# Encoder values made with tokens on the partitions, and their head layout assembled by DMA through DRAM

## The reference, cut to what matters

```python
keys = jnp.concatenate([past, x], axis=1)
q = (x @ Wq.T + bq).reshape(B, T, HEADS, HEAD_DIM)
k = (keys @ Wk.T + bk).reshape(B, T + H, HEADS, HEAD_DIM)
v = (keys @ Wv.T + bv).reshape(B, T + H, HEADS, HEAD_DIM)
...
attn = jax.nn.softmax(scores, axis=-1)
o = jnp.einsum('bhqk,bkhd->bqhd', attn, v).reshape(B, T, C)
o = o @ Wo[l].T + bo[l]
```

## Time and profile before

| what | value |
|---|---|
| time, median of 3 runs | 821.11 us (820.96 to 821.4) |
| span of the profiled execution | 819.1 us |
| TensorE (PE) busy | 801.5 us, 98% of the span |
| VectorE (DVE) busy | 633.9 us, 77% |
| ScalarE (ACT) busy | 460.6 us, 56% |
| GpSimd (POOL) busy | 251.6 us, 31% |
| DMA | 88.36 MB, 30.4% of 16 engines' span |

### The profile page before, as it was taken

How to read it: one execution, slowest core, us unless ns; L and a number is a source line. 1 busy time by engine, 2 the same in 40 slices (tenths; PEclk the granted TensorE clock), 3 DMA queues, 4 the chain that set the end, 5 groups by cost and what they waited for, 6 DMA issues and landing times.

```text
span 819.1 us, 16629 instructions
## 1 busy us (share of the span) xinstructions
PE 801.5 (98%) x6060; PEld 751.4 (92%) x6060; DVE 633.9 (77%) x1287; ACT 460.6 (56%) x829; POOL 251.6 (31%) x297
## 2 busy tenths in 40 slices
PE   9999999999999999999999999999999999999988
PEld 8998789999999999899999989999998999999758
DVE  5786693778778876778797887878778787876796
ACT  4386424433333336585786777667687767745421
POOL 0002120410111100364366147335525623633020
PEclk9999999999999999999999999999999999999999
DMA  5010946998889812010210021031012103010001
GB/s 191 1 52 1 373 124 253 328 323 310 317 309 337 321 53 107 1 40 14 100 44 0 17 98 38 13 102 38 4 39 72 38 13 102 26 82 1 1 0 30
DMA packets 18290, 88.36 MB, mean 108 GB/s; under 512 B 3120, under 2 KB 7472, under 8 KB 12240
## 3 DMA queue, kind: packets, MB, share of 16 engines
q1 hardware_dynamic: 18256, 87.90, 30.4%
HBM read 85.05 MB, written 2.84 MB: 107 GB/s over the span
## 4 chain that ended last, share of the span: by engine, by line
PE 47%; issue 23%; POOL 18%; DVE 8%; ACT 3%; DMA 1%; POOLq 0%; SPq 0%; DVEq 0%; ACTq 0%
PE bank L1139 14%; POOL W_L L2000 7%; PE bank L1176 6%; POOL HF_L L2058 4%; POOL arena L1981 3%; POOL WQKV_L L2000 3%; PE bank L746 2%; PE bank L872 2%; PE bank L1185 2%; PE bank L722 2%; PE bank L1049 2%; PE bank L788 1%; POOL SQ L2019 1%; PE bank L1123 1%; PE bank L1490 1%
## 5 line engine op out<-in xcount | busy, mean ns | idle before, releaser
L1139 PE MATMUL bank<-arena 128*128 (+1 forms) x1024 | 117.8, 274 | 0.0
L1139 PEld LDWEIGHTS bank<-arena 128*128 128x128 f32 x1024 | 117.4, 192 | 0.0
L1981 POOL TENSOR_TENSOR arena<-arena,srec 111x456 f32<-111x456 f32 x56 | 52.3, 962 | 125.1 <-DVE srec L2153 125.1
L2000 POOL TENSOR_TENSOR W_L<-LW,W_H 128x256 fp32r<-128x256 f32 x96 | 68.5, 752 | 36.9 <-DVE XHL L2589 33.5
L2058 POOL TENSOR_TENSOR HF_L<-arena,HF_H 128x296 fp32r<-128x296 f32 x48 | 43.8, 937 | 76.7 <-ACT HF_H L1896 76.7
L788 PE MATMUL bank<-XHL,W_H 128*128 128x296 f32 x288 | 65.1, 307 | 0.0
L1896 ACT ACTIVATE arena<-bank,vec 128x296 f32<-128x296 f32 x96 | 48.8, 509 | 20.4 <-PE bank L788 15.4
L2012 POOL TENSOR_TENSOR QW<-QW,arena x14 | 22.4, 1600 | 119.0 <-DVE QW L2490 65.6
L1330 PE MATMUL bank<-HF_L,W_H 128*128 128x296 f32 x192 | 57.4, 299 | 0.0
L1330 PE MATMUL bank<-HF_H,W_H 128*128 128x296 f32 x192 | 57.4, 299 | 0.0
L1330 PE MATMUL bank<-HF_H,W_L 128*128 128x296 f32 x192 | 57.3, 299 | 0.0
(11 more groups left out here) (276 smaller groups left out, 2205.4 us busy)
## 6 DMA issues: line engine op xcount, KB each, us to landing
arena<-ew_in SPq DMA_DIRECT2D x16, 2048.0 KB, 9.0
arena<-ew_in SPq DMA_DIRECT2D x16, 1024.0 KB, 7.0
LW<-lw_in SPq DMA_DIRECT2D x12, 1024.0 KB, 5.0
arena<-route SPq DMA_DIRECT2D x32, 185.0 KB, 3.2
LW<-lw_in SPq DMA_DIRECT2D x6, 768.0 KB, 4.3
fp_weights<-arena SPq DMA_DIRECT2D x1, 2048.0 KB, 6.4
arena<-fp_weights SPq DMA_DIRECT2D x1, 2048.0 KB, 7.2
arena<-patches_in SPq DMA_DIRECT2D x2, 864.0 KB, 7.4
```

Source lines behind the costliest of these rows:

```text
L1139: last = mm(o[:, m * CAP:(m + 1) * CAP], w[:, kc, mi * P:(mi + 1) * P], xg(kc, e), start=(kc == 0), stop=(kc == C - 1))
L1981: nc.gpsimd.tensor_tensor(v, v, srec[0:QROWS, s:s + 2, :].unsqueeze(3).to_broadcast([QROWS, 2, C * JH, KEYS]), ALU.mult).then_inc(p_ready, 1)
L2000: last = nc.gpsimd.tensor_tensor(low[:, cols], value[:, cols], high[:, cols], ALU.subtract)
```

## The change

V of a half is made token-major: the stationary operand is now 104 token columns of x (13 tokens of 8 images), the moving one the 256 V columns of the weights. For this the columns of the encoder's activations are ordered token by token, image within token (`by_key` in place of `images`), so that 104 neighbouring columns are 13 tokens of all 8 images; three such tiles start at tokens 0, 12 and 24. V takes 18 products with 256 moving columns (`value_rows`), 12 of them ahead of the layer norm's variance and 6 behind it; the 16 transposes, the mask products on VectorE and the threefold copy are gone. Q and K chunk 0 come first, V last. ScalarE copies the rows out of PSUM twice per half (104 rows by 512 and by 256 columns). SyncE then stores them to a DRAM tensor `spread` of [128, 8, 256] that is zeroed once at the start: 9 DMAs per half, one for each of 3 tiles and 3 slots, on 104, 96 and 96 rows, with 6, 5 and 5 runs of 16 numbers (64 bytes) in each row, 4736 runs in all. When they have landed, SyncE loads the whole 1 MB into `Ve` with one DMA, which `values` waits for. The Q/K/V weights of the next layer are issued behind that load. In chunk 1 the head slots are rotated by one (`krot`), since 8 heads are no multiple of 3. `set_kbias` moves into the A phase, behind the softmax sums.

```diff
@@ -120,11 +120,10 @@
-    att("w", 0, 1)
...
         att("k", c)
-    att("v", 0, 1, 2, 3)
+    att("w", 0, 1)
@@ -136,6 +135,10 @@
+KEY_STARTS = (0, 12, 24)
+KEY_RUN = 13
+VROWS = KEY_RUN * HB
@@ -246,6 +250,7 @@
         VT = v_.rearrange("p (c b g k) -> p c b g k", c=C, b=HB, g=JH)
+        v3 = VT.rearrange("p c b g k -> p (c b g k)")[0:VROWS, 0:3 * D].rearrange("p (i n) -> p i n", i=3)
@@ -357,6 +362,11 @@
+        spread = nc.dram_tensor("spread_values", (P, HB, D), F32, kind="Internal").ap()
+        spread_rows = spread.rearrange("r b n -> (r b) n").rearrange("x (e d) -> x e d", d=HD)
+        SPREAD_DMAS = len(KEY_STARTS) * JH
@@ -462,6 +473,10 @@
+        def half_count(l, h):
+            return l * 2 + h
@@ -516,6 +531,9 @@
+        def by_key(ap):
+            return ap.rearrange("p (t b) -> p b t", t=T)
@@ -620,6 +638,8 @@
             sp.dma_start(lvec[:, :, :], a["lvec"].rearrange("l p n -> p l n")).then_inc(ld_lvec, 16)
+            sp.wait_ge(setup_done, 1)
+            sp.dma_start(spread, OB[:, 0, 0, 0:D].unsqueeze(1).to_broadcast([P, HB, D])).then_inc(spread_zeroed, 16)
@@ -691,16 +711,44 @@
-            with sp.Fori(1, LAYERS) as l:
-                sp.wait_ge(filled["v"], nth("v", 7, l))
+            def store_value_rows(l, h):
+                sp.wait_ge(w_ready, nth("w", 2 * h + 1, l + 1))
+                if not (isinstance(l, int) and l + h == 0):
+                    sp.wait_ge(spread_loaded, half_count(l, h) * 16)
+                for i, k0 in enumerate(KEY_STARTS):
+                    lo = 0 if i == 0 else (KEY_STARTS[i - 1] + KEY_RUN - k0) * HB
+                    for g in range(JH):
+                        row = (g * KEYS + k0) * HB
+                        sp.dma_start(spread_rows[row + lo:row + VROWS, g::JH, :],
+                                     v3[lo:VROWS, i, :].rearrange("p (e d) -> p e d", d=HD)[:, g::JH, :]
+                                     ).then_inc(spread_stored, 16)
+            def load_value_rows(l, h):
+                sp.wait_ge(spread_stored, half_count(l, h) * (SPREAD_DMAS * 16) + SPREAD_DMAS * 16)
+                sp.wait_ge(filled["o"], nth("o", 3, l + 1) if h else nth("o", 7, l))
+                sp.dma_start(Ve[:, 0:HB, :], spread).then_inc(spread_loaded, 16)
+            sp.wait_ge(spread_zeroed, 16)
+            store_value_rows(0, 0)
+            load_value_rows(0, 0)
+            for l in range(1, LAYERS):
+                store_value_rows(l - 1, 1)
+                load_value_rows(l - 1, 1)
...
                 load_rest(l, "wo", LW_AT["wo"], WO_N, ld_wo)
+                store_value_rows(l, 0)
+                load_value_rows(l, 0)
...
+            store_value_rows(LAYERS - 1, 1)
+            load_value_rows(LAYERS - 1, 1)
@@ -804,10 +852,23 @@
-            def project_v(r, plan, h, pairs, high_count, low_count):
-                two_products(r, plan, [("w", 2 * h + c) for c in range(C)], [pairs(c) for c in range(C)],
-                             high_count, low_count)
+            def value_rows(r, plan, h, which):
+                for part, weights in ((XH, (WQKV_H, WQKV_L)), (XL, (WQKV_H,))):
+                    for kc in range(C):
+                        for i in which:
+                            key = ("w", 2 * h + i // 2)
+                            opens = part is XH and kc == 0 and i % 2 == 0
+                            if opens:
+                                free_bank(r, plan, key)
+                            o = bank_of(plan, key)[0:VROWS, (i % 2) * D:(i % 2 + 1) * D]
+                            keys = part[:, h, kc, KEY_STARTS[i] * HB:KEY_STARTS[i] * HB + VROWS]
+                            for w in weights:
+                                last = mm(o, keys, w[:, kc, 2 * D:3 * D],
+                                          start=opens and w is WQKV_H, stop=part is XL and kc == C - 1,
+                                          skip_group_check=True)
+                last.then_inc(filled["w"], 1)
@@ -864,8 +925,10 @@
                     free_bank(r, plan, key, ("t", 2 * g4 + 1))
-                    if c == 0:
+                    if c == 0 and plan.first:
                         pe.wait_ge(v_ready, nth("v", 4 * h + 3, r))
+                    elif c == 0:
+                        pe.wait_ge(spread_loaded, half_count(r - 1, h) * 16 + 16)
@@ -1346,7 +1408,8 @@
-                    project_v(rx, plan, hx, lambda c: qkv_pairs(2, c), high_count, low_count)
+                    two_products(rx, plan, [("q", 2 * hx), ("k", 2 * hx)], [qkv_pairs(0, 0), qkv_pairs(1, 0)],
+                                 high_count, low_count)
@@ -1357,9 +1420,7 @@
                 if x:
-                    if y:
-                        pe.wait_ge(proj_added, nth("p", 2 * hy, ry))
-                    queries_or_keys(0, "q")
+                    queries_or_keys(1, "q")
@@ -1370,8 +1431,10 @@
                 if x:
-                    queries_or_keys(0, "k")
-                    queries_or_keys(1, "q", "k")
+                    queries_or_keys(1, "k")
+                    if entry:
+                        ln_bcast_of(LN_ENC, 1)
+                    value_rows(rx, plan, hx, (0, 1))
@@ -1379,9 +1442,7 @@
                 if x:
-                    if entry:
-                        ln_bcast_of(LN_ENC, 1)
-                    turn_v(rx, plan, hx)
+                    value_rows(rx, plan, hx, (2,))
@@ -1552,6 +1613,16 @@
+            def value_rows_out(l, plan, h):
+                for k in range(2):
+                    act.wait_ge(filled["w"], nth("w", 2 * h + k, l + 1))
+                    if k == 0 and not (isinstance(l, int) and l + h == 0):
+                        act.wait_ge(spread_stored, half_count(l, h) * (SPREAD_DMAS * 16))
+                    o = bank_of(plan, ("w", 2 * h + k))[0:VROWS, 0:(2 - k) * D]
+                    f(v3[:, 2 * k:3 - (1 - k), :].rearrange("p i n -> p (i n)"), o, ACT.Copy).then_inc(w_ready, 1)
@@ -1862,28 +1934,28 @@
                     p0 = HB // 2 * hx
-                    values_out(rx, plan, hx)
+                    act.wait_ge(kbias_ready, lx + 1)
+                    def keys(c):
+                        act.wait_ge(filled["k"], nth_enc("k", 2 * hx + c, rx))
+                        o = bank_of(plan, ("k", 2 * hx + c))
+                        for g in range(JH):
+                            last = f(Ke[:, 0, c, :, g, 0:T], by_key(o[:, 0:NHALF]), ACT.Identity,
+                                     bias=kbias[:, c * JH + g:c * JH + g + 1], scale=krot[:, c + g:c + g + 1])
+                        last.then_inc(k_ready, 1)
+                    keys(0)
...
                 if x:
-                    act.wait_ge(kbias_ready, lx + 1)
-                    def keys(c):
-                        act.wait_ge(filled["k"], nth_enc("k", 2 * hx + c, rx))
-                        o = bank_of(plan, ("k", 2 * hx + c))
-                        for g in range(JH):
-                            last = f(Ke[:, 0, c, :, g, 0:T], images(o[:, 0:NHALF]), ACT.Identity,
-                                     bias=kbias[:, c * JH + g:c * JH + g + 1], scale=cst("kmask", g, g + 1))
-                        last.then_inc(k_ready, 1)
-                    keys(0)
+                    keys(1)
...
                 if x:
-                    keys(1)
+                    value_rows_out(lx, plan, hx)
@@ -2160,7 +2232,7 @@
                     def take(s, lo, hi):
-                        dst = images(OB[lo:hi, h, c, :])[:, 4 * (g4 % 2):4 * (g4 % 2) + 4, :]
+                        dst = by_key(OB[lo:hi, h, c, :])[:, 4 * (g4 % 2):4 * (g4 % 2) + 4, :]
@@ -2176,6 +2248,7 @@
             v.memset(eps_sq[:, :], EPS * EPS)
+            v.memset(OB[:, 0, 0, 0:D], 0.0)
@@ -2235,6 +2308,8 @@
                     v.tensor_scalar(pos, pos, prm("in_b", c), None, ALU.add)
+                for k in range(2):
+                    v.tensor_copy(krot[:, k * JH:(k + 1) * JH], cst("kmask"))
@@ -2564,7 +2639,6 @@
                 ln_centre(LN_ENC, h)
-            clear_value_pads()
@@ -2573,7 +2647,7 @@
                                                 ALU.mult, ALU.mult))
-                    v.tensor_tensor(images(XD[:, h, c, :]), images(CN[:, h, c, :]),
+                    v.tensor_tensor(by_key(XD[:, h, c, :]), images(CN[:, h, c, :]),
@@ -2592,14 +2666,14 @@
             ln_recip(LN_ENC, 1)
-            dve.wait_ge(cleared, 2)
...
                 for c in range(C):
-                    v.tensor_scalar(kbias[:, c * JH:(c + 1) * JH], cst("kmask"), lv(l, "bqkv", C + c), None, ALU.mult)
-                    last = v.tensor_scalar(Ke[:, 0, c, :, :, T], per_image(cst("kmask")), lv(l, "bqkv", C + c), None,
+                    slots = krot[:, c:c + JH]
+                    v.tensor_scalar(kbias[:, c * JH:(c + 1) * JH], slots, lv(l, "bqkv", C + c), None, ALU.mult)
+                    last = v.tensor_scalar(Ke[:, 0, c, :, :, T], per_image(slots), lv(l, "bqkv", C + c), None,
@@ -2691,12 +2765,13 @@
                 for c in range(C):
```

(24 more changed lines are left out.)

## The result

The changed kernel takes 826.26 us (median of 4 runs, 825.93 to 826.69) against 821.13 us for the kernel before beside it: a ratio of 1.0059, 95% interval [1.0045, 1.0073]. It is **slower by 0.6%**, where 813.5 us was forecast.

The account below looks back on a forecast made before the run. TensorE, busy 98% of an 819.1 us span, was taken as the bound. Eleven phases at -0.84 us (-9.2) plus 1.6 in the first gave 811.5 of span, 813.5 us median; own range 810 to 818, 8 in 10 809.5 to 836.

Parts of the forecast that it names:

- The front of the phase: TensorE between variance and broadcast: six products replace 16 transposes, broadcast 0.84 us earlier in each of eleven phases.
- so I cost the strided write at nothing: VectorE's writes into `OB`, now 32 bytes apart: no added time.
- a rival of their own: VectorE's six Q instructions before the inverse: strided PSUM reads cost double, 832.9 us; chance 0.20.
- `set_kbias` moves off the start of the B phases into a wait of VectorE for the feed-forward result; nothing: VectorE, `set_kbias` moved out of the B phases' start: no gain and no cost.
- The DMA path: Stores and load of value rows through DRAM: 9.2 plus 5.0 us, hidden except in the first phase.
- the packet: Time per 64-byte store run on a DMA engine: taken as 24 ns, between 14 and 36.
- +1.6 us: First phase, without feed-forward work as cover: values wait for the load, 1.6 us longer.
- The second rival: SyncE's wait for the stores: small stores slow at 48 ns per packet, values late, 872 us; chance 0.16.
- the third: No change: packets of 29 to 30 ns, or reads with about half the penalty, cancel the gain, 821 us; chance 0.08.
- The sum: Whole span: -9.2 us from eleven phases' fronts and +1.6 from the first phase, 811.5 us of span.

Follow-up runs that it names:

- experiment 6: The changed kernel with 33 more VectorE instructions behind its last add, three for each of eleven read and write patterns, other engines idle: 838.25 us, one run.
- experiment 2: The changed kernel with the instructions that write `OB` going image innermost, in runs of 4 neighbouring numbers: 815.42 us, 0.9929 of the kernel before.
- experiment 1: The changed kernel with `set_kbias` ahead of the four row sums of the A phases instead of behind them: 820.52 us, 0.9988 of the kernel before.
- experiment 4: The kernel before with `set_kbias` alone moved to where the change has it, behind the A phases' row sums: 827.26 us, 1.0070 of the kernel before.
- experiment 7: The changed kernel with 24 more VectorE instructions at its end, four kinds, first with GpSimd idle, then beside fourteen GpSimd adds: 846.87 us, one run.
- experiment 3: The changed kernel with both `set_kbias` ahead of the row sums and the `OB` writes image innermost: 809.42 us, 0.9856 of the kernel before.
- experiment 5: The changed kernel with its nine stores of value rows issued twice, first to an array nothing reads: 832.26 us, 1.0129 of the kernel before.

## Why the prediction was wrong

**The front of the phase: right, and a little small.** Variance to broadcast was to fall from 2.46 us to 1.62 and fell to 1.46 (the six products with the change of kind were put at 0.90 us and took 0.77); mean to variance kept its length (3.16 against 3.15 us), as the prediction had asked. Without the two losses the five A and five B phases gain 1.14 and 1.04 us where 0.84 was forecast. Only the eleventh phase does not (see the sum).

**Step that failed: "so I cost the strided write at nothing".** It rested on the earlier trace rows: 24 numbers 152 bytes apart take 243 ns where 3 neighbours take 222, 1 ns for each number more. The comparison was of two counts, not of two steps. The price of a step is what it adds to the same count without it, and no row gave that for 24 numbers. By experiment 6, 148 neighbours from SBUF take 290 ns, so one number more costs about (290 - 222) / 145 = 0.47 ns; the row's 1 ns was already twice that, and it was read as the normal rate. Measured, the step adds 0.11 us to each take: 0.86 us in the first phase, 0.90 in the A and 0.98 in the B phases, 0.8 at the end, 11.1 together (experiment 2). And its place was never looked up: behind nine of these writes stands `ln_rs`, for which TensorE already waited 0.17 us in each of ten phases before, so that there was no slack to hide anything in.

The prediction looked for the danger on the other side. It gave strided reads of PSUM a rival of their own, with a chance of 0.20, and that rival falls: the six Q instructions still take 3.05 us, in VectorE's timeline of the B phase:

```profile
385.50 3.05 DVE L2811 TENSOR_SCALAR arena<-bank,lvec,qmask 128x296 f32<-128x296 f32 x6
```

The rule cited there (the Trainium skill, SBUF — State Buffer, Door 1: The DMA port swizzle) speaks of lines of 16 bytes in SBUF that want at least two hits each. Experiment 6 agrees for VectorE's fp32 writes: two numbers per 16 bytes at 0.37 us, one at 0.47. So the rule bore on the writes into `OB`, 32 bytes apart in SBUF; the prediction held it against the reads of PSUM alone. For PSUM the Trainium skill gives lines of 8 bytes there and speaks of matmuls; 3.05 us for the six shows no such price for VectorE's reads.

**Step that failed: "`set_kbias` moves off the start of the B phases into a wait of VectorE for the feed-forward result; nothing".** That wait existed, 0.36 us for an issue and 0.23 for TensorE, but it did not hold four instructions; and no row was asked what they cost there. In the B phases they took 0.65 us (381.90 to 382.55 before); beside GpSimd's normalising they take 2.5 us. Measured, 1.1 us in each of five A phases, 5.6 to 5.7 us (experiments 1 and 4). That nothing comes back in the B phases was right. The trace of before held the warning, in VectorE's timeline: the same `RSUM` took 1.01 us beside GpSimd's normalising and 0.47 us at the start of the B phase.

```profile
371.10 1.01 DVE L2706 TENSOR_TENSOR RSUM<-R 128x296 f32<-128x296 f32 x1
...
381.52 0.47 DVE L2706 TENSOR_TENSOR RSUM<-R 128x296 f32<-128x296 f32 x1
```

The Trainium skill (SBUF — State Buffer, Who interferes with whom) calls this an exclusive lock on a port pair that VectorE shares with GpSimd, and leaves out instructions with a single SBUF input outside the two-port modes; experiment 7 agrees with the lock (0.47 to 1.09 us for two SBUF inputs) and with the exception (0.53 us unchanged for one SBUF input beside one in PSUM). The adds over three numbers have a single SBUF input and still went from 0.23 to 0.99 us; by that rule they ran in a two-port mode, which no run here shows.

**The DMA path: hidden, as forecast; the packet was priced too high.** 9.2 us were forecast from the stores' first issue to their landing; it was 6.7 us in the first phase, 7.9 in the A phase shown and 6.0 to 6.1 in most. SyncE's nine issues alone take 4.6 us of that, so by the prediction's own sum, 320 packets on the busiest engine and 1.5 us for the way, a packet costs at most some 14 ns (an estimate), its lowest row and not the 24 that it took. So the first phase never paid its +1.6: TensorE does not wait for the load there in the change (0.36 us in experiment 3), and with the takes mended that phase is 26.50 us in experiment 2 and 26.74 in experiment 3, 0.54 and 0.30 shorter than before. The second rival (872 us) has its mechanism refuted by these landings and by experiment 5, and the third, which needed half of one of these two, falls with them.

**The sum.** Forecast -9.2 + 1.6 = -7.6. Measured in the phases of experiment 3: 5 x (-1.14) + 5 x (-1.04) - 0.30 = -11.2, then -0.2 at the end and -0.4 ahead of the encoder, 11.8 us of span. The change as it stands adds to that 11.1 for the writes and 5.7 for `set_kbias`: +5.0, and its span is 5.5 longer. The rest is no more than the scatter ahead of the encoder: in seven profiled kernels whose front part is the changed one, the encoder begins anywhere between 316.85 and 318.52. The end holds the eleventh phase and gains 0.2 us instead of 1.1. The likely cause, read from the traces and not tried: `add_stream`, which now reads the stream 32 bytes apart in SBUF, takes 1.41 us for its two instructions where it took 0.96, once in the last A phase and once behind it. The prediction had no term for it.

**Luck.** 826.3 us lies inside the range of 8 in 10, 809.5 to 836. But that range was stretched so far for rivals whose mechanisms the runs refute; the two losses that brought the time there were terms that the prediction had put at nothing.

## What to carry to other kernels

A new layout is paid for by whoever writes it: cost the strided side per number against a contiguous row of the same count, and look up what stands behind those instructions in their engine's order. If the step can't be avoided, let the innermost loop run over the written neighbours where the other operand is read from PSUM: that stride cost nothing here, while a read step of 8 in SBUF cost as much as a write step (0.06 us for 148 numbers). Before a small VectorE instruction is moved, see whether GpSimd is busy there; four instructions of 0.2 us on SBUF operands can cost a GpSimd instruction each.

## What the runs showed of the hardware

- VectorE writing fp32 to SBUF from PSUM, 148 numbers per partition: 0.37 us at a step of 1 or 2 numbers, 0.47 to 0.48 at 4 or 8. From SBUF to SBUF: 0.29 us, and 0.35 with a step of 8 on either side.
- VectorE reading PSUM with a step of 3, 8 or 111 numbers: no longer than neighbours (0.37 us; 3.05 us for six; 367 ns).
- A VectorE instruction with SBUF operands alone, beside GpSimd's adds of 0.98 us: 0.23 becomes 0.99, 0.47 becomes 1.09 in two of three. With a PSUM operand: unchanged.
- Nine DMAs with 4736 runs of 64 bytes to DRAM land 6.0 to 7.9 us after the first issue, eighteen 10.8 to 12.1.
- After TensorE had waited 4.7 us in the first phase of experiment 5, its granted clock was 0.50 (1.2 GHz) in the window from 341 to 345, and 32 value products took 6.20 us instead of 3.80.
